# A filler product in front of every transposed score of the 16-dim-head attentions

## The chip, the cores and the metric

The kernel runs on one core of one Trainium2 chip. The metric is the device time of one execution in microseconds (us); several executions are made and their median is compared. The profile is of one further execution.

## The reference, cut to what matters

The program is a decoder of four layers over 4 batches of 512 tokens with 256 features. Each layer has an attention, a cross attention and a feed-forward part, twelve sublayers in all. Three of them (the cross attention of layer 0, the attentions of layers 1 and 3) have 16 heads of 16 dimensions and a softmax over 512 keys; layers 1 and 3 mask the future, layer 0 doesn't. Layer 1 reads:

```python
q, k, v = map(split_heads, (q, k, v))        # 16 heads of 16 dimensions
q = q * dh ** (-0.5)
sim = jnp.einsum('bhid,bhjd->bhij', q, k)
if causal:
    sim = jnp.where(causal_mask, mask_value, sim)
m = jax.lax.stop_gradient(jnp.max(sim, axis=-1, keepdims=True))
e = jnp.exp(sim - m)
num = jnp.einsum('bhij,bhjd->bhid', e, v)
den = jnp.sum(e, axis=-1, keepdims=True) + eps
out = num / den
```

The cross attention of layer 0 divides the scores by 16 and masks nothing; layer 3 rotates q and k first.

## The kernel before, in words

One function, `softmax_heads` (L545), computes these three sublayers. The outer program runs the layers one after the other for a batch in a hardware loop over the four batches, so the trace has twelve calls: the first, third, fifth and seventh without a mask (layer 0), the second, fourth, sixth and eighth causal (layer 1), the last four causal (layer 3, with rotation). Each call is one block in which each engine has a program written out by hand, tied to the others by semaphores.

Heads are taken in eight pairs. A pair lies stacked on the 128 partitions, one head on 64 rows each; q and k are split into a high and a low part, so that a product of 64 rows gives an exact score. For each pair the work has two halves:

- Row scores: `row_scores(p, qt)` (L654) makes, for a tile of 128 queries, the scores against the keys in two products of 64 rows, one for each head, into a ring of three PSUM banks (0 to 2). VectorE takes the row maxima (L785), splits -max in two parts (L795, L797), TensorE transposes them (`put`, L669) and VectorE adds them to q's spare rows (L801).
- Transposed scores: `col_scores(n)` (L682) makes, for a tile of 128 keys, the scores with keys on the partitions and -max already in them, again two products of 64 rows, into banks 3 and 4 or 5 and 6 by turns. ScalarE takes the exp (L880). `weigh(g, kt)` (L701) multiplies by v, four heads side by side in column strips of 32 (p @ v, fp32).

With a mask, products of narrow halves (L659, L687) add the mask's diagonal tile, and the products cover only the columns that count, 128 to 512 of them.

The order on TensorE is that of the loop at L742: for a step i of pair p it issues the row scores of pair p, then the transposed scores of pair p - 2, then p @ v of the step before where that step's pair is an odd one, then, once in a pair, the put. In the first two pairs stacking (L633) and values (L641) take the place of the transposed scores. Behind the last row scores there are eight steps with transposed scores alone, among which the sums (L713), the spreading of 1/sum (L720) and the output projection (L727) are issued.

`col_scores(n)` waits for the exp two steps earlier (`probs_done`, n - 1), which frees the banks that it writes.

A helper, `keep_warm` (L101), issues products whose output nobody reads; it is used in other places of the kernel, among them the tail of each of these calls (L321). Its product is

```python
pe.matmul(self.psum[:, bank, :], self.select[:, 0, :], self.select[:, 0:BANK // P, :], start=True, stop=True)
```

that is 128 rows by 128 columns of weights against 512 columns of a constant, in the type of the stacking products (L633).

Of the kernel before, what the change touches and what calls it, by code (L numbers as in the profile page):

```python
# [544 lines left out]
def softmax_heads(net, W, x, qsrc, ksrc, scale, causal, guard, norm, start, jobs=None, rope=None):  # L545
# [15 lines left out]
    def put_slot(p):  # L561

        return tiles * (p + 1) + p + (PUT_AT if p + 1 < PAIRS else 0)
# [8 lines left out]
    with ExitStack() as ctx:  # L572
# [14 lines left out]
        with net.block() as (block, sem):  # L587
# [34 lines left out]
            def _(pe):  # L622
# [49 lines left out]
                def col_scores(n):  # L672
                    p, kt = divmod(n, steps)
                    if kt == 0:
                        pe.wait_ge(row_read, put_slot(p) + 1)
                    if n >= 2:
                        pe.wait_ge(probs_done, n - 1)
                    else:
                        pe.wait_ge(stacked, outputs)
                    lo = kt * P if causal else 0  # L680
                    for j, half in enumerate(halves):
                        mm = pe.matmul(net.psum[:, 3 + 2 * (n % 2) + j, lo:T], ks[half, p, kt * P:(kt + 1) * P], qs[half, p, lo:T],  # L682
                                       start=True, stop=not causal)
                    if causal:
                        for i in range(2):
                            for j, half in enumerate(halves):
                                mm = pe.matmul(net.psum[:, 3 + 2 * (n % 2) + j, lo:lo + P], net.half_ident[half, i, :],  # L687
                                               net.half_causal_cols[half, i, :], start=False, stop=i == 1)
                    mm.then_inc(colscores_done, 1)
# [52 lines left out]
                for p in range(PAIRS + lag):  # L742
                    for i in range(steps):
                        if p < PAIRS:
                            row_scores(p, i)
                        if p < 2:
                            if i % 2 == 0:
                                stack(2 + 3 * p + i // 2)
                            else:
                                values(2 * p + i // 2)  # L750
                            if i == 3:
                                stack(4 + 3 * p)
                        if p >= lag:
                            n = (p - lag) * steps + i
                            col_scores(n)
                            last_p, last_kt = divmod(n - 1, steps)
                            if n and last_p % 2:
                                weigh(last_p // 2, last_kt)
                        if 1 <= p <= PAIRS and i == (PUT_AT // 2 - 1 if p < PAIRS else 0):
                            put(p - 1)  # L760
                        if p >= PAIRS:
                            at = (p - PAIRS) * steps + i
                            if at in (1, 3, 5):
                                totals(at // 2)
                            if at in (2, 4, 6):
                                spread_inverse(at // 2 - 1)
                            if at in (3, 5, 7):
                                project(at // 2 - 1)
# [1956 lines left out]
```

## Time and profile before

| | |
|---|---|
| median of 3 runs | 4101.51 us (4095.73 to 4104.26) |
| the profiled execution | 4108.26 us |
| its span, first to last instruction | 4106.3 us |
| mean granted TensorE clock | 0.891 |
| TensorE busy | 3326.1 us (81%), 18369 products |
| VectorE busy | 2006.9 us (49%) |
| ScalarE busy | 1238.4 us (30%) |
| GpSimd busy | 427.5 us (10%) |

Busy time of TensorE (PE) counts products from their issue to a modelled end, and neighbouring products overlap, so a high share doesn't say that the array is always streaming. The granted clock is 1.00 at the higher level (2.4 GHz) and 0.50 at the lower; a mean between them says what share of a stretch had which. PEld is the weight load of a product. L numbers are lines of the kernel before. DVE is VectorE, ACT is ScalarE. A timeline line with "x2" merges two products that start within a few ns of each other (one for each head).

### The profile page before, as it was taken

To read this page: it belongs to the slowest core of one execution; us is meant where nothing else is said; L and a number is where in the kernel's file an instruction comes from. 1 tells how busy PE (TensorE), PEld (TensorE's weight loads), DVE (VectorE), ACT (ScalarE), POOL (GpSimd) and SP (SyncE) were. 2 spreads that over 40 slices of the span, in tenths; PEclk is the share of its full clock that TensorE was granted. 3 is DMA by queue.
4 is the path that set the end of the run, shared out by engine and by line. 5 is a ranking of instruction groups with operands and counts; after the bars stand their busy time and mean duration, and the time that the engine had idled before them with its cause. 6 is when DMAs were issued, how large, how long until landed. Compare 5 with 4: busy or idle time off the path is not lost. (4 is left out here: it accounts for less than half of the span.)

```text
span 4106.3 us, 48913 instructions
## 1 busy us (share of the span) xinstructions
PE 3326.1 (81%) x18369; PEld 2148.7 (52%) x18369; DVE 2006.9 (49%) x4645; ACT 1238.4 (30%) x2331; POOL 427.5 (10%) x413
## 2 busy tenths in 40 slices
PE   4878789678869967886996788699496888888888
PEld 2465555436555543655554365555395555454555
DVE  3664446466454646645554564555211535344343
ACT  1413226151322524132252413235131323222132
POOL 1010101111010111001010100101102001010100
PEclk9889899898989988898998889899698999898989
DMA  4000100200010020001002000100585020201101
GB/s 171 6 8 16 76 20 1 90 13 13 22 66 11 1 90 13 13 22 66 11 1 89 13 13 22 66 11 1 206 304 201 1 87 9 87 8 53 43 27 66
DMA packets 53212, 209.29 MB, mean 51 GB/s; under 512 B 4976, under 2 KB 37616, under 8 KB 41328
## 3 DMA queue, kind: packets, MB, share of 16 engines
q1 hardware_dynamic: 48128, 198.85, 13.0%
q0 software_dynamic: 1536, 4.20, 0.3%
q8 instruction: 158, 2.59, 0.3%
q10 hardware_dynamic: 3312, 3.02, 0.2%
q14 instruction: 78, 0.64, 0.1%
HBM read 186.89 MB, written 19.16 MB: 50 GB/s over the span
## 5 line engine op out<-in xcount | busy, mean ns | idle before, releaser
L785 DVE TENSOR_REDUCE nmax<-psum 128x1 f32<-128x512 f32 (+3 forms) x768 | 391.4, 551 | 157.4 <-PE psum L659 124.2
L307 POOL TENSOR_TENSOR rstd<-rstd,consts 128x1 f32<-128x1 f32 x160 | 88.2, 551 | 2204.6 <-DVE rstd L281 2204.6
L880 ACT ACTIVATE probs_odd<-psum 128x1024 f32<-128x1024 f32 x192 | 155.7, 811 | 271.7 <-PE psum L687 189.3
L108 PE MATMUL psum<-select 128*128 128x512 f32 x520 | 192.0, 502 | 49.8 <-PEq L120 49.8
L654 PE MATMUL psum<-ks,qs 64*128 64x512 f32 (+3 forms) x768 | 174.0, 447 | 61.8 <-DVE nmax L785 60.2
L329 ACT ACTIVATE xc<-psum 128x256 f32<-128x256 f32 x144 | 55.4, 385 | 543.6 <-PE psum L314 543.6
L1726 ACT ACTIVATE exps<-exps,nmax 128x512 f32<-128x512 f32 x256 | 183.3, 716 | 71.4 <-DVE nmax L1672 70.9
L1672 DVE CUSTOM_DVE_ANT_0 exps<-psum,mrows 128x512 f32<-128x512 f32 x256 | 166.1, 689 | 67.7 <-PE psum L1619 64.6
L880 ACT ACTIVATE probs_even<-psum 128x1024 f32<-128x1024 f32 x192 | 153.8, 811 | 111.2 <-PE psum L687 74.7
L654 PEld LDWEIGHTS psum<-ks,qs 64*128 64x128 f32 x768 | 75.1, 188 | 201.1 <-DVE nmax L785 120.8
L682 PE MATMUL psum<-qs,ks 64*128 64x512 f32 (+3 forms) x768 | 165.2, 422 | 6.8 <-ACT ks L846 5.9
L701 PE MATMUL psum<-probs_even,v 128*32 128x512 f32 (+3 forms) x768 | 170.2, 523 | 0.0
L701 PE MATMUL psum<-probs_odd,v 128*32 128x512 f32 (+3 forms) x768 | 170.2, 523 | 0.0
L108 PEld LDWEIGHTS psum<-select 128*128 128x128 f32 x520 | 114.7, 239 | 75.8 <-issue 55.6
L314 PE MATMUL psum<-consts,xn 128*128 128x128 f32 x320 | 71.6, 308 | 92.1 <-DVE xn L287 91.9
L1630 PE MATMUL psum<-consts,exps 128*128 128x128 f32 x1024 | 138.9, 279 | 3.9 <-DVE arena L1680 1.5
L1630 PEld LDWEIGHTS psum<-consts,exps 128*128 128x128 f32 x1024 | 109.5, 141 | 56.0 <-ACT exps L1726 39.8
L1641 PE MATMUL psum<-arena,v 128*64 128x512 f32 x512 | 134.8, 608 | 3.6 <-ACT arena L1739 3.2
L727 PE MATMUL psum<-arena,o 128*128 128x256 f32 x384 | 128.9, 494 | 9.3 <-DVE o L828 9.3
L458 PE MATMUL psum<-k,q 128*128 128x512 f32 (+3 forms) x192 | 90.3, 632 | 46.9 <-PEq L120 46.9
L1182 PE MATMUL psum<-qkv_high,xc_parts 128*128 128x512 f32 x384 | 119.2, 390 | 1.3 <-PEq L120 1.3
L2252 PE MATMUL psum<-arena,hidden 128*128 128x256 f32 x512 | 119.6, 379 | 0.0
(395 smaller groups left out, 6987.3 us busy)
## 6 DMA issues: line engine op xcount, KB each, us to landing
arena<-in_w SPq DMA_DIRECT2D x23, 1028.0 KB, 7.7
arena<-in_w SPq DMA_DIRECT2D x23, 1024.0 KB, 7.9
arena<-in_pack_L_ffn SPq DMA_DIRECT2D x4, 5184.5 KB, 15.0
arena<-in_pack_L_xattn SPq DMA_DIRECT2D x4, 4744.0 KB, 14.8
arena<-in_pack_L_ffn SPq DMA_DIRECT2D x4, 4120.0 KB, 12.3
arena<-in_pack_L_attn SPq DMA_DIRECT2D x5, 2432.0 KB, 9.0
arena<-in_pack_L_attn SPq DMA_DIRECT2D x9, 1280.0 KB, 5.7
arena<-ternary SPq DMA_DIRECT2D x4, 2056.0 KB, 7.7
```

What stands on the lines that cost most here:

```text
L108: pe.matmul(self.psum[:, bank, :], self.select[:, 0, :], self.select[:, 0:BANK // P, :], start=True, stop=True)
L654: mm = pe.matmul(net.psum[:, bank_of(s + j), 0:w], qs[half, p, qt * P:(qt + 1) * P], ks[half, p, 0:w], start=True, stop=not causal)
L682: mm = pe.matmul(net.psum[:, 3 + 2 * (n % 2) + j, lo:T], ks[half, p, kt * P:(kt + 1) * P], qs[half, p, lo:T], start=True, stop=not causal)
L701: mm = pe.matmul(net.psum[u * PITCH:(u + 1) * PITCH, 7, lo:T], v[:, kt, 4 * g + u, :], probs((2 * g + u // 2) * steps + kt)[:, u % 2, lo:T ...
L727: mm = pe.matmul(net.psum[:, 1 + t // 2, t % 2 * D:(t % 2 + 1) * D], o[:, g, t * P:(t + 1) * P], W["wo"][:, g * D:(g + 1) * D], start=g == ...
L785: dve.tensor_reduce(nmax[:, p, qt, n % 2:n % 2 + 1], net.psum[:, bank_of(s), 0:w], AX.X, ALU.max, negate=True).then_inc(row_read, 1)
L880: act.activation(probs(n)[:, :, lo:T], net.psum[:, first:first + 2, lo:T], ACT.Exp, scale=scale).then_inc(probs_done, 1)
L1630: mm = pe.transpose(net.psum[:, 4 + j, kt * P:(kt + 1) * P], e[:, m % ring, kt * P:(kt + 1) * P], net.ident)
L1641: mm = pe.matmul(net.psum[half, 6, :], v[:, kt, 2 * p + j, :], turned[p % 2][:, kt, j, :], start=kt == 0, stop=kt == NT - 1, tile_position ...
L1672: dve.tensor_tensor_reduce(e[:, m % ring, :], net.psum[:, 2 * (u % 2) + j, :], mrows[:, u % NT, :], -DK ** -0.5, 1e20, ALU.add, ALU.min, n ...
L1726: act.activation(e[:, m % ring, :], e[:, m % ring, :], ACT.Exp, bias=nmax[:, m % ring:m % ring + 1], scale=-1.0, accum_out=total[:, p % 2, ...
L2252: mm = pe.matmul(output(t), hidden[:, n, t * P:(t + 1) * P], W["up"][:, n * D:(n + 1) * D], start=n == 0 and t % 2 == 0, stop=n == chunks ...
```

## The change

`col_scores` issues one product of `keep_warm` behind its wait and in front of its own products. It is written to the first of the two banks of this step, which the transposed score of the first head overwrites. Nothing else is touched. There are 32 transposed-score steps in a call, so 384 products more in all.

```diff
--- before.py
+++ after.py
@@ -677,6 +677,7 @@
                         pe.wait_ge(probs_done, n - 1)
                     else:
                         pe.wait_ge(stacked, outputs)
+                    net.keep_warm(pe, 1, bank=3 + 2 * (n % 2))
                     lo = kt * P if causal else 0
                     for j, half in enumerate(halves):
                         mm = pe.matmul(net.psum[:, 3 + 2 * (n % 2) + j, lo:T], ks[half, p, kt * P:(kt + 1) * P], qs[half, p, lo:T],
```

## Rows read from the trace of the kernel before

**Rows 1.** Page, part 5: line, engine, operation, tiles, count, busy us, mean ns, idle before

```profile
L682 PE MATMUL psum<-qs,ks 64*128 64x512 f32 (+3 forms) x768 | 165.2, 422 | 6.8 <-ACT ks L846 5.9
```

**Rows 2.** Windows, third call: us, busy us (count) by engine, clock, DMA

```profile
847.10:853.16 6.06, 3.52 (x25) 1.65 (x21) 5.74 (x12) 4.34 (x6) 0.00 (x0) 1.00 0.00 0
853.50:861.00 7.50, 7.50 (x56) 2.24 (x52) 6.29 (x13) 4.10 (x4) 0.00 (x0) 1.00 0.01 2
866.20:869.60 3.40, 3.16 (x14) 0.85 (x14) 2.07 (x4) 1.54 (x2) 0.00 (x0) 0.50 0.00 0
```

**Rows 3.** Timeline, TensorE, third call (not causal): start us, us, line, tiles [idle before]

```profile
847.10 0.50 PE L654 MATMUL psum<-ks,qs 64*128 64x512 f32 x2
...
848.38 0.49 PE L654 MATMUL psum<-ks,qs 64*128 64x512 f32 x2 [0.56 <-DVE nmax L785]
...
849.07 0.63 PE L669 MATMUL psum<-consts,spread 128*128 128x128 f32 x4
850.26 0.49 PE L654 MATMUL psum<-ks,qs 64*128 64x512 f32 x2 [0.56 <-DVE nmax L785]
...
853.16 0.50 PE L654 MATMUL psum<-ks,qs 64*128 64x512 f32 x2 [0.78 <-DVE nmax L785]
853.50 0.40 PE L682 MATMUL psum<-qs,ks 64*128 64x512 f32 x2
853.82 0.62 PE L701 MATMUL psum<-probs_even,v 128*32 128x512 f32 x2
...
854.82 0.50 PE L654 MATMUL psum<-ks,qs 64*128 64x512 f32 x2
```

**Rows 4.** Timeline of TensorE, first call, row scores beside 128-row products

```profile
101.61 0.50 PE L654 MATMUL psum<-ks,qs 64*128 64x512 f32 x2
102.04 0.50 PE L633 MATMUL psum<-xc_parts,select 128*128 128x512 f32 x1
...
102.60 0.39 PE L633 MATMUL psum<-xc_parts,select 128*128 128x512 f32 x1
102.83 0.39 PE L633 MATMUL psum<-low,select 128*128 128x512 f32 x1
103.15 0.50 PE L654 MATMUL psum<-ks,qs 64*128 64x512 f32 x2
```

**Rows 5.** Timeline of VectorE, third call, the step with the put

```profile
850.13 0.68 DVE L801 TENSOR_TENSOR qs<-qs,psum 128x512 fp32r<-128x512 f32 x1
```

**Rows 6.** Groups by line in four waiting steps of the fourth call (causal)

```profile
L654 PE MATMUL psum<-ks,qs 64*128 64x384 f32 (+3 forms) x8 | 1.6, 406 | 1.3 <-DVE nmax L785 1.3
```

**Rows 7.** Timeline of TensorE, third call, a step behind the last row scores

```profile
876.38 1.02 PE L713 MATMUL psum<-consts,o 128*128 128x4 f32 x8 [0.44 <-DVE qs L801]
```

**Rows 8.** Windows, first to twenty-fifth transposed score of each call, and their sum

```profile
833.47:873.42 39.95, 32.31 (x206) 11.73 (x206) 34.99 (x64) 25.00 (x26) 0.00 (x0) 0.96 0.00 1
1042.08:1077.36 35.28, 31.20 (x394) 17.62 (x394) 25.08 (x63) 17.70 (x26) 0.00 (x0) 1.00 0.01 2
1543.44:1586.31 42.87, 35.22 (x207) 12.23 (x208) 35.00 (x64) 25.01 (x26) 0.00 (x0) 0.88 0.00 1
...
sum 453.68, PE 390.91 PEld 191.66 DVE 340.76 ACT 245.37 POOL 0.00; mean PE 32.58 PEld 15.97 DVE 28.40 ACT 20.45 POOL 0.00
```

**Rows 9.** Windows, twenty-fifth to last transposed score of each call, and their sum

```profile
873.42:891.31 17.89, 16.64 (x111) 10.73 (x107) 4.80 (x12) 7.81 (x9) 0.00 (x0) 1.00 0.00 1
1077.36:1099.00 21.64, 20.64 (x138) 14.71 (x134) 5.09 (x13) 5.83 (x8) 0.00 (x0) 0.76 0.00 1
...
1791.85:1812.49 20.64, 19.30 (x138) 13.65 (x135) 5.08 (x13) 5.83 (x8) 0.00 (x0) 0.83 0.00 1
...
sum 244.80, PE 230.90 PEld 160.03 DVE 59.92 ACT 77.46 POOL 0.00; mean PE 19.24 PEld 13.34 DVE 4.99 ACT 6.46 POOL 0.00
```

**Rows 10.** Windows, the 45 us behind the last transposed score of each call

```profile
180.55:225.55 45.00, 27.43 (x113) 19.85 (x113) 22.31 (x71) 12.69 (x17) 15.36 (x9) 0.70 0.08 30
...
1099.00:1144.00 45.00, 37.83 (x146) 23.25 (x146) 16.28 (x40) 7.10 (x16) 4.54 (x5) 0.89 0.13 47
```

## The prediction

> **What bounds the kernel now.** I began with the page's groups to size the edit: the transposed scores are 768 products, two heads to a step, so 384 steps, 32 in each of twelve calls (three attentions, four batches) [rows 1]. The page's shares over the whole span can't say what 384 more products are worth, so I cut the third call, one without a causal mask, into windows. The reader is to see two kinds of step there. In steps without p @ v, VectorE is busy 5.74 us of 6.06 with the row maxima and TensorE 3.52; in steps with p @ v, TensorE is busy 7.50 us of 7.50 [rows 2]. The timeline says the same by waits: before the row scores of the first kind TensorE sat idle 0.56 to 0.78 us until a maximum was taken; in the second kind no row has an idle time [rows 3]. So a longer TensorE step is free in the first kind and lengthens the second by its full amount.
>
> Then the clock. For 3.40 us of this call the grant was 0.50, the lower of its two levels (1.2 GHz) [rows 2]. Over the first 24 steps, a call at 0.96 took 39.95 us and the same call at 0.88 took 42.87 [rows 8]; causal calls mostly hold 1.00 there, at 35.28. In the last eight steps it is the causal calls that fall, to 0.76 and 0.83 [rows 9]. That is what fillers could give back.
>
> **The cost of one filler.** It goes in after the step's existing wait and before its two products, so the same wait now holds the filler's weight load; no wait is added, no DMA, SP or POOL instruction, and the bank is one whose reader that wait covers. ACT's exp and the next p @ v come later by the filler, but exp (one per step) has a whole step before p @ v asks for it.
>
> The price lies in the shape. The filler uses 128 rows; the row scores in front of it and the transposed scores behind it use 64. Same-shape neighbours pack densely: 128-row products stand 0.23 us apart (102.60 to 102.83) [rows 4], and row score to transposed score takes 0.34 (853.16 to 853.50) [rows 3]. Across a change of shape it is 0.43 from the start of a row score to a 128-row product (101.61 to 102.04), and 0.32 from a 128-row product whose load was hidden to the row score behind it (102.83 to 103.15) [rows 4]. The difference, 0.11, is a load that is no longer hidden. With the filler a step reads: row score 0.43, filler 0.32 + 0.11 = 0.43, transposed score 0.32 + 0.11 = 0.43, together 1.29. Now it is 0.66 (853.16 to 853.82) [rows 3]. So **0.63 us** where nothing hides it. The bounds: 0.23, if both loads hide as between equal shapes, and 0.63; I take 0.63, since the rows that put these two shapes side by side all show it. At the lower clock it costs more: the last rival has that.
>
> On this the Trainium skill speaks the other way ("TensorE: Matmul & The Clock Gate", Part 2, Step-by-step): a weight load is pulled ahead of products in flight if it goes to the background buffer. By that alone a filler would cost its 0.23. The trace agrees between equal shapes only; it is the first rival.
>
> **Step by step, full clock.** Of a call's first 24 steps, 11 are followed by p @ v and bound by TensorE: 11 x 0.63 = 6.9 us. The 13 others wait for VectorE. Without a mask, the waits of 0.56 to 0.78 about absorb 0.63, except where -max is put into q: the put starts 0.69 after its row score now (848.38 to 849.07) [rows 3] and at 1.29 after the change, and being 0.63 long would end at 848.38 + 1.29 + 0.63 = 850.30. VectorE's addition, which waits for it, starts at 850.13 now [rows 5]: 0.2 late, once in each of three pairs, 0.6. With the mask, four such steps have only 1.3 us of idle time together [rows 6] against 4 x 0.63 = 2.5: 1.2 at most; starts follow each other closer than the modelled ends that idle time counts from, so I take 0.9, three times: 2.7.
>
> In the last eight steps there are no row scores. The first follows p @ v, whose weights are 32 columns wide: one more shape, 0.43. The other seven follow 128-row products, so only 0.23 is added; three of them stand before a wait like the 0.44 us for VectorE [rows 7] and are free: 4 x 0.23. Together 1.35.
>
> Sum: 6.9 + 0.6 + 1.35 = 8.9 us for each of four calls without a mask, 6.9 + 2.7 + 1.35 = 10.9 for each of eight causal ones: 35.6 + 87.2 = **+123 us**.
>
> **What the clock gives back.** First 24 steps: extrapolating 0.88 and 0.96 to 1.00 gives 42.87 - 12 x 0.365 = 38.5 without a mask; the twelve calls sum to 453.68, less 4 x 38.5 and 8 x 35.28: 17.4 us [rows 8]. Last eight: 17.89 without a mask; causal, 21.64 at 0.76 and 20.64 at 0.83 extrapolate to 18.2; 244.80 - 4 x 17.89 - 8 x 18.2 = 27.6 [rows 9]. So 45 us at most, 0 at least. A filler adds 512 columns to each of the sparse steps. I take all of the 17 (it is mostly the calls without a mask that fall there, those with TensorE busy 3.52 of 6.06 us in the waiting steps [rows 2]) and half of the rest: **-31 us**.
>
> The same page's closing table asks only that TensorE not idle long between bursts if the clock is to hold. By that rule nothing would fall here, where no idle time shown is over 0.78 us, and the gain would be 0. The trace has the falls, and it decides.
>
> Net +92 us. The profiled execution took 4108.26 us (span 4106.3); the median of the runs is 6.75 lower. 4108.3 + 92 = 4200, as a median **4193 us**.
>
> **Rivals.**
> 1. The loads hide after all, and a paid filler costs 0.23. Waiting steps take it free, so 11 + 5 in each call pay: 192 x 0.23 = 44 us; less 31, 4108.3 + 13, as a median 4115 (4101 to 4146 for 45 to 0 recovered). For it: equal shapes do this [rows 4]. Against: the 0.43 beside row scores.
> 2. Faster: the clock. A paid filler at 0.23 breaks even when all 45 us come back (45 / 192 = 0.23), and the gain is decided by whether the clock also holds behind the calls. In the 45 us there it was granted 0.70 to 0.89 [rows 10], so 10 to 27 us at the lower level each, some 220 over twelve. If a quarter of that is spared, that is 55 us at some 0.44 each (2.92 us between 0.88 and 0.96 of 41 us [rows 8], 6.6 us more at the lower level), 24: 44 - 45 - 24 = -25, as a median 4077. Against: the shape price again, and no filler is added behind the calls.
> 3. The filler doesn't do its work: the clock falls as before. Then +123, and the roughly 120 us at the lower level (from the windows' grants) hold some 40 fillers that cost up to twice as much, near +15: +138, as a median 4240. For it: calls whose TensorE is busier than 90% in the last steps still fall [rows 9].
>
> **How the numbers follow.** My forecast (loads exposed, part of the clock back): 0.64, a median of 4165 to 4224. Rival 1: 0.15; rival 2: 0.07; rival 3: 0.14. The range runs from rival 1's middle to rival 3: 4112 to 4240; it leaves out rival 2 and half of rival 1. About 0.2% (8 us) is what a measurement of this kernel can tell from no change. Faster by more: rival 2 and a little of rival 1, 0.08. Within: 0.05, from rival 1. Slower: 0.87.
>
> **What would show it.** 384 more products on line 108. Starts of filler to transposed score 0.43 apart, row score to p @ v 1.29 (0.89 under rival 1). The idle time before row scores in waiting steps nearly gone, that of VectorE in steps with p @ v longer. First 24 steps near 46 us without a mask and near 45 with one, granted clock near 1.00; last eight steps near 19 to 21 us. If row score to p @ v stays near 0.89, the shape price is wrong and with it the sign of the result is open; if the grant in these windows doesn't move, rival 3 holds.

## The result, and the profile after

The changed kernel took 4159.47 us (median; 4150.42 to 4160.94), the kernel before 4099.32 us in the same comparison: a ratio of 1.0141, 95% interval 1.0123 to 1.016. It is slower by 60 us.

From the page of the changed kernel: its span, then groups (line, engine, operation, tiles, count, busy us, mean ns, idle before and what ended it). Behind the edit, lines are one higher.

```profile
span 4158.1 us, 49681 instructions
...
L108 PE MATMUL psum<-select 128*128 128x512 f32 x904 | 383.0, 499 | 54.3 <-PEq L120 48.3
...
L654 PE MATMUL psum<-ks,qs 64*128 64x512 f32 (+3 forms) x768 | 169.3, 436 | 6.5 <-DVE nmax L786 3.9
```

The same groups of the kernel before:

```profile
L108 PE MATMUL psum<-select 128*128 128x512 f32 x520 | 192.0, 502 | 49.8 <-PEq L120 49.8
...
L654 PE MATMUL psum<-ks,qs 64*128 64x512 f32 (+3 forms) x768 | 174.0, 447 | 61.8 <-DVE nmax L785 60.2
```

The products on line 108 went from 520 to 904: the 384 fillers are there. Row scores (L654) had 61.8 us of idle time in front of them and have 6.5. VectorE's idle time before its maxima (L785, now L786) rose from 157.4 to 201.3. What happened to the clock is read from windows of the stage, below.

TensorE in the third call, a call without a mask (start us, duration us, engine, line, operation, tiles, count, idle before):

```profile
852.30 0.50 PE L654 MATMUL psum<-ks,qs 64*128 64x512 f32 x2
852.73 0.50 PE L108 MATMUL psum<-select 128*128 128x512 f32 x1
853.16 0.50 PE L683 MATMUL psum<-qs,ks 64*128 64x512 f32 x2
853.59 0.62 PE L702 MATMUL psum<-probs_even,v 128*32 128x512 f32 x2
...
855.87 0.51 PE L654 MATMUL psum<-ks,qs 64*128 64x512 f32 x2
...
857.16 0.66 PE L669 MATMUL psum<-consts,spread 128*128 128x128 f32 x4
857.76 0.50 PE L654 MATMUL psum<-ks,qs 64*128 64x512 f32 x2
...
859.29 0.51 PE L654 MATMUL psum<-ks,qs 64*128 64x512 f32 x2 [0.17 <-DVE nmax L786]
```

The first four rows are a step followed by p @ v: row score, filler, transposed score and p @ v start 0.43 us apart, 1.29 in all, where [rows 3] had 0.66. The others are steps that used to wait for VectorE: 855.87 to 857.76 goes without a pause, and where a wait is left it is 0.17 (859.29) in place of 0.56 to 0.78 [rows 3].

The weight loads (PEld) of the first of these steps, and below them that of the transposed score in the kernel before:

```profile
852.73 0.19 PEld L108 LDWEIGHTS psum<-select 128*128 128x128 f32 x1 [0.24 <-issue]
853.16 0.19 PEld L683 LDWEIGHTS psum<-qs,ks 64*128 64x128 f32 x2 [0.24 <-issue]
```

```profile
853.26 0.19 PEld L682 LDWEIGHTS psum<-qs,ks 64*128 64x128 f32 x2
```

A load takes 0.19 us. Before, the transposed score's load started 0.24 ahead of its product (853.50 [rows 3]), while the row score was under way. Now the filler's load and the transposed score's start with their products (852.73 and 853.16), 0.24 after the load before them ended: neither is hidden.

The windows answer to [rows 8] and [rows 9] (stretch, its length, busy us and count for PE, PEld, DVE, ACT and POOL, granted clock, DMA). First to twenty-fifth transposed score, then their sum over the twelve calls:

```profile
838.38:884.65 46.27, 45.27 (x231) 17.46 (x230) 35.49 (x65) 25.35 (x26) 0.00 (x0) 1.00 0.00 1
1055.72:1099.11 43.39, 43.07 (x421) 22.54 (x420) 26.21 (x64) 17.85 (x26) 0.00 (x0) 1.00 0.01 1
...
sum 532.17, PE 525.68 PEld 250.04 DVE 351.53 ACT 246.82 POOL 0.00; mean PE 43.81 PEld 20.84 DVE 29.29 ACT 20.57 POOL 0.00
```

Twenty-fifth to last:

```profile
884.65:903.47 18.82, 18.35 (x115) 11.72 (x114) 4.24 (x10) 7.66 (x8) 0.00 (x0) 1.00 0.00 1
1099.11:1117.39 18.28, 17.87 (x143) 12.49 (x143) 4.26 (x11) 5.83 (x8) 0.00 (x0) 1.00 0.00 1
...
sum 221.66, PE 216.41 PEld 146.92 DVE 51.16 ACT 76.91 POOL 0.00; mean PE 18.03 PEld 12.24 DVE 4.26 ACT 6.41 POOL 0.00
```

All twenty-four windows are at a granted clock of 1.00 now (2.4 GHz). The first 24 steps took 532.17 us against 453.68 [rows 8], 78.5 more; the last eight 221.66 against 244.80 [rows 9], 23.1 less. Together +55.4; the span grew by 51.8, so the rest of the program lies within 4 us of what it was. In one and the same change the first part pays and the second part earns. The first stretch ends at the twenty-fifth transposed score, so it also holds the filler in front of that, the first of the last eight steps.

### The profile page after: what moved, and what is told of

Read it like the earlier page. It is cut to its first block and busy times, and to the rows that moved or that the text cites. A ratio compares the mean times of both kernels' runs of the same rounds, so it can differ in the third digit from the quotient of the medians.

```text
span 4158.1 us, 49681 instructions
## 1 busy us (share of the span) xinstructions
PE 3441.8 (83%) x18753; PEld 2190.0 (53%) x18753; DVE 2009.3 (48%) x4645; ACT 1241.1 (30%) x2331; POOL 427.4 (10%) x413
## 5 line engine op out<-in xcount | busy, mean ns | idle before, releaser
L786 DVE TENSOR_REDUCE nmax<-psum 128x1 f32<-128x512 f32 (+3 forms) x768 | 391.3, 551 | 201.3 <-PE psum L659 161.1
L108 PE MATMUL psum<-select 128*128 128x512 f32 x904 | 383.0, 499 | 54.3 <-PEq L120 48.3
L108 PEld LDWEIGHTS psum<-select 128*128 128x128 f32 x904 | 186.0, 217 | 131.6 <-issue 78.6
L329 ACT ACTIVATE xc<-psum 128x256 f32<-128x256 f32 x144 | 55.4, 385 | 540.3 <-PE psum L314 540.3
L654 PE MATMUL psum<-ks,qs 64*128 64x512 f32 (+3 forms) x768 | 169.3, 436 | 6.5 <-DVE nmax L786 3.9
L702 PE MATMUL psum<-probs_odd,v 128*32 128x512 f32 (+3 forms) x768 | 161.1, 498 | 0.0
L702 PE MATMUL psum<-probs_even,v 128*32 128x512 f32 (+3 forms) x768 | 161.1, 498 | 0.0
L654 PEld LDWEIGHTS psum<-ks,qs 64*128 64x128 f32 x768 | 73.4, 185 | 123.5 <-issue 79.0
L728 PE MATMUL psum<-arena,o 128*128 128x256 f32 x384 | 115.6, 453 | 9.4 <-DVE o L829 9.4
L683 PEld LDWEIGHTS psum<-qs,ks 64*128 64x128 f32 x768 | 71.4, 183 | 96.0 <-issue 96.0
```

The costliest lines, as they stand in the source:

```text
L654: mm = pe.matmul(net.psum[:, bank_of(s + j), 0:w], qs[half, p, qt * P:(qt + 1) * P], ks[half, p, 0:w], start=True, stop=not causal)
L702: mm = pe.matmul(net.psum[u * PITCH:(u + 1) * PITCH, 7, lo:T], v[:, kt, 4 * g + u, :], probs((2 * g + u // 2) * steps + kt)[:, u % 2, lo:T ...
L728: mm = pe.matmul(net.psum[:, 1 + t // 2, t % 2 * D:(t % 2 + 1) * D], o[:, g, t * P:(t + 1) * P], W["wo"][:, g * D:(g + 1) * D], start=g == ...
L786: dve.tensor_reduce(nmax[:, p, qt, n % 2:n % 2 + 1], net.psum[:, bank_of(s), 0:w], AX.X, ALU.max, negate=True).then_inc(row_read, 1)
```

## The experiments

All diffs are against the changed kernel. Times are medians, ratios are to the kernel before.

### 64-row fillers in place of 128-row ones

```diff
-                    net.keep_warm(pe, 1, bank=3 + 2 * (n % 2))
+                    for j, half in enumerate(halves):
+                        pe.matmul(net.psum[:, 3 + 2 * (n % 2) + j, :], net.select[half, 0, :], net.select[half, 0:BANK // P, :], start=True, stop=True)
```

> The filler as a pair of 64-row products, one into each of the two banks, so that it has the shape of the row scores before it and of the transposed scores behind it; as many columns stream as before. Theory (most of the price of 0.63 us is the change of shape): row score to p @ v takes 0.34 + 0.23 + 0.32 = 0.89 us in place of 1.29, the first 24 steps take about 41 us without a mask and 38 with one (46.3 and 43.4 with the 128-row filler), the clock stays at 1.00, and the time falls by some 66 us from 4159 to about 4093. Rival (the price is that of a product that writes the bank which the next one overwrites, whatever its shape): step 1.29 or more, 4159 or more. Second rival (64-row pairs don't keep the clock up): step 0.89, but grants near 0.9 again and about 4125.

Measured: 4094.25 us, ratio 0.9994 (0.9985 to 1.0003). TensorE in a step followed by p @ v of the third call (L681 the pair of fillers, L684 the transposed score, L703 p @ v), then the first 24 steps of the third call and of the fourth, a causal one:

```profile
848.62 0.50 PE L654 MATMUL psum<-ks,qs 64*128 64x512 f32 x2
848.96 0.39 PE L681 MATMUL psum<-select 64*128 64x512 f32 x2
849.19 0.40 PE L684 MATMUL psum<-qs,ks 64*128 64x512 f32 x2
849.51 0.62 PE L703 MATMUL psum<-probs_even,v 128*32 128x512 f32 x2
```

```profile
826.27:867.53 41.26, 36.36 (x256) 16.07 (x254) 35.44 (x64) 25.24 (x26) 0.00 (x0) 1.00 0.00 1
1037.29:1075.06 37.77, 36.47 (x444) 20.34 (x442) 25.78 (x62) 17.74 (x26) 0.00 (x0) 1.00 0.01 2
```

Row score to filler 0.34, filler to transposed score 0.23, to p @ v 0.32: 0.89, as the theory gave. The weight load of the transposed score starts ahead of its product again (848.96 to 849.19). The clock is at 1.00 in all calls. The first 24 steps of the twelve calls sum to 467.91 us, 64 less than with the 128-row filler (532.17), for the same streaming in the neighbours' shape: the change of shape was the larger part of the price. A write to the bank that is overwritten next costs nothing that shows: 0.23 is what neighbours of equal shape take in [rows 4].

### One filler of a quarter of the columns, and two fillers

```diff
-                    net.keep_warm(pe, 1, bank=3 + 2 * (n % 2))
+                    pe.matmul(net.psum[:, 3 + 2 * (n % 2), 0:P], net.select[:, 0, :], net.select[:, 0, :], start=True, stop=True)
```

> The 128-row filler with 128 columns in place of 512, in all 32 steps. Theory (0.40 of the 0.63 us is the change of shape, only the streaming shrinks): row score to p @ v about 1.13 us in place of 1.29, so 0.47 for a filler of a quarter of the columns; with the clock at 1.00 some 4128, with the clock falling as before some 4170. Rival (the price goes with the columns): a step of about 0.82 us, 4060 to 4105.

```diff
-                    net.keep_warm(pe, 1, bank=3 + 2 * (n % 2))
+                    net.keep_warm(pe, 2, bank=3 + 2 * (n % 2))
```

> Two 128-row fillers in place of one, in all 32 steps. Theory (the price of the first is mostly the change of shape, a second of the same shape costs its 0.23 us): row score to p @ v 1.52 us in place of 1.29, first 24 steps near 50.5 us without a mask and 48.5 with one, about 4232. Rival (each filler costs 0.63): a step of 1.92 us, over 4330.

Measured, one run each: 4156.17 us with the short filler, 4230.93 us with two. TensorE in a step with p @ v, first with the short filler (L680), then with two (L108, merged into one row):

```profile
853.75 0.50 PE L654 MATMUL psum<-ks,qs 64*128 64x512 f32 x2
854.17 0.33 PE L680 MATMUL psum<-select 128*128 128x128 f32 x1
854.43 0.51 PE L683 MATMUL psum<-qs,ks 64*128 64x512 f32 x2
854.86 0.62 PE L702 MATMUL psum<-probs_even,v 128*32 128x512 f32 x2
```

```profile
865.47 0.49 PE L654 MATMUL psum<-ks,qs 64*128 64x512 f32 x2
865.89 0.73 PE L108 MATMUL psum<-select 128*128 128x512 f32 x2
866.55 0.49 PE L683 MATMUL psum<-qs,ks 64*128 64x512 f32 x2
866.98 0.62 PE L702 MATMUL psum<-probs_even,v 128*32 128x512 f32 x2
```

Row score to p @ v is 1.11 with the short filler and 1.51 with two (865.47 to 866.98), against 1.29 with one and 0.66 with none. So 0.45 for a filler of 128 columns, 0.63 for one of 512, and 0.22 for the second: the price is a fixed part of about 0.40, paid for the change of shape, and the streaming on top. Both rivals, in which the price goes by columns or by fillers, are out.

The short filler's windows hold something else (first 24 steps of the third and fourth call; last eight of the fourth):

```profile
840.51:888.78 48.27, 46.08 (x232) 18.53 (x232) 35.68 (x66) 25.25 (x26) 0.00 (x0) 0.89 0.00 1
1062.20:1102.31 40.11, 39.30 (x420) 22.61 (x419) 25.72 (x62) 17.84 (x26) 0.00 (x0) 1.00 0.01 2
```

```profile
1102.31:1119.92 17.61, 16.67 (x143) 12.50 (x143) 4.47 (x11) 5.83 (x8) 0.00 (x0) 1.00 0.00 1
```

Without a mask the clock still fell: 0.93, 0.89, 0.86 and 0.93 in the four calls, where the kernel before has 0.92, 0.96, 0.88 and 0.88, and the third call took 48.27 us. In the last eight steps it fell in six calls of twelve (nine before). So the step lengthened nearly as the theory said, and less came back: the time was close to the changed kernel's, by another route.

### Fillers in the waiting steps alone

```diff
-                    net.keep_warm(pe, 1, bank=3 + 2 * (n % 2))
+                    if n < 24 and (n == 0 or (n - 1) // steps % 2 == 0):
+                        net.keep_warm(pe, 1, bank=3 + 2 * (n % 2))
```

> The 128-row filler only in the 13 of the first 24 steps that aren't followed by p @ v; none in the other steps and none in the last eight. Theory (there it lies in time in which TensorE waits for VectorE): first 24 steps about 39 us without a mask and 36.5 with one at a clock of 1.00, last eight as in the kernel before (17.9 to 22.2, grants 0.76 to 1.00), together about 4094. Rival (the clock needs the fillers beside p @ v too): without a mask grants of 0.88 to 0.96 as before, about 4110.

Measured: 4135.56 us, ratio 1.0096 (1.0081 to 1.0112). Both numbers for the total were too low. First 24 steps of the third and the fourth call, then the last eight of the third and the sum of the twelve:

```profile
831.98:871.79 39.81, 38.16 (x219) 14.42 (x219) 34.66 (x63) 24.86 (x26) 0.00 (x0) 1.00 0.00 1
1046.33:1084.91 38.58, 36.67 (x408) 19.99 (x407) 25.10 (x62) 17.50 (x26) 0.00 (x0) 1.00 0.01 2
```

```profile
871.79:894.02 22.23, 21.25 (x110) 14.17 (x107) 4.81 (x12) 7.79 (x9) 0.00 (x0) 0.77 0.00 1
...
sum 256.54, PE 242.67 PEld 169.05 DVE 60.02 ACT 77.39 POOL 0.00; mean PE 20.22 PEld 14.09 DVE 5.00 ACT 6.45 POOL 0.00
```

Without a mask it did what was expected: 39.81 us at 1.00, in place of up to 42.87. So the fillers that keep the clock in the first 24 steps are those in the waiting steps; those beside p @ v are not needed for it. With a mask it cost 38.58 against 35.28 [rows 8], 3.3 for three groups of four, 1.1 each, near the upper bound of 1.2. Two stretches of the fourth call show where: four steps with p @ v and the four waiting steps behind them, first in the kernel before, then in this run, with the one wait that this run has there:

```profile
1047.84:1054.56 6.72, 6.62 (x84) 3.33 (x84) 4.44 (x12) 2.85 (x5) 0.00 (x0) 1.00 0.01 2
1054.56:1059.91 5.35, 4.06 (x56) 2.68 (x52) 4.37 (x12) 3.26 (x6) 0.00 (x0) 1.00 0.00 2
```

```profile
1052.72:1059.90 7.18, 6.62 (x90) 3.32 (x88) 4.32 (x12) 2.96 (x5) 0.00 (x0) 1.00 0.01 2
1059.90:1065.89 5.99, 5.89 (x60) 3.51 (x58) 4.51 (x12) 3.03 (x5) 0.00 (x0) 1.00 0.00 1
```

```profile
1054.03 0.62 PE L703 MATMUL psum<-probs_even,v 128*32 128x512 f32 x2 [0.46 <-ACT probs_odd L882]
```

The waiting steps themselves take 0.64 us more (5.99 for 5.35). The other 0.46 stands in front of the first p @ v, which now waits for ScalarE's exp. And in the last eight steps, which have no filler here, the clock fell in all twelve calls, also in those without a mask, where it held in three of four before: 256.54 us in place of 244.80. Why it fell in more of them is not settled.

### Fillers in the last eight steps alone

```diff
-                    net.keep_warm(pe, 1, bank=3 + 2 * (n % 2))
+                    if n >= 24:
+                        net.keep_warm(pe, 1, bank=3 + 2 * (n % 2))
```

> The 128-row filler only in the last eight of the 32 steps of a call. Theory (in these the filler follows 128-row products and costs 0.23 at most, half of it hidden, while the clock there falls in nine calls of twelve): the first 24 steps as in the kernel before (sum 453.7 us over the calls), the last eight 18.8 us without a mask and 18.3 with one at 1.00, sum 222 in place of 244.8: about 23 us less than before, 4076. Rival (the clock in the last eight is decided by what runs before them): grants of 0.76 to 0.83 stay, sum near 255, about 4110.

Measured: 4080.78 us, ratio 0.9965 (0.9952 to 0.9979). First 24 steps of the fourth call, then the sum of the last eight over the twelve calls:

```profile
1036.31:1072.06 35.75, 31.68 (x397) 17.83 (x397) 25.55 (x63) 17.70 (x26) 0.00 (x0) 1.00 0.01 2
```

```profile
sum 221.70, PE 216.46 PEld 146.90 DVE 56.46 ACT 76.91 POOL 0.00; mean PE 18.04 PEld 12.24 DVE 4.71 ACT 6.41 POOL 0.00
```

221.70 us, to within 0.1 of the changed kernel's sum, at 1.00 in all calls. What runs before doesn't decide it; the fillers in these steps do. This part of the change alone is a gain of 0.35%, 15.7 us. The first 24 steps without a mask were granted 0.88 to 0.92 here, 0.88 to 0.96 before. With a mask the fourth call took 35.75 us in them for 35.28 [rows 8], at 1.00 both times: 0.47 is the price of the filler in front of the twenty-fifth transposed score, at which the window ends. Twelve of these are some 5.5 us, so that of the 23.1 us the last eight steps earn about 18.

### Fillers beside p @ v alone

```diff
-                    net.keep_warm(pe, 1, bank=3 + 2 * (n % 2))
+                    if n < 24 and n and (n - 1) // steps % 2:
+                        net.keep_warm(pe, 1, bank=3 + 2 * (n % 2))
```

> The 128-row filler only in the 11 of the first 24 steps that are followed by p @ v. The causal calls hold the clock there with no filler, so they show the price alone. Theory of the prediction (0.63 us in each of these steps, and 0.3 to 1.1 more for four waiting steps, which add up): 35.3 + 6.9 = 42.2 us in the first 24 steps with a mask. Rival (the prices don't add: what the fillers cost in one kind of step is partly time that VectorE uses to get ahead, so it shortens the waiting steps behind it): about 40 us, so that the waiting steps' 3.3 us from the run with fillers there alone and these 4.8 make the 8.1 that the change costs. In total near 4125 to 4145, with grants below 1.00 in the last eight steps.

Measured: 4178.98 us in one run, outside the range that was given. First 24 steps of the third and fourth call:

```profile
847.82:897.74 49.92, 42.29 (x217) 15.10 (x217) 35.75 (x66) 24.98 (x26) 0.00 (x0) 0.90 0.00 1
1069.11:1110.21 41.10, 37.24 (x405) 20.00 (x405) 25.88 (x63) 17.69 (x26) 0.00 (x0) 1.00 0.01 2
```

With a mask 41.10: 5.8 us for eleven fillers, 0.53 each. That lies between the two theories. The two stretches of the fourth call again, in this run, and the second of them in the changed kernel:

```profile
1074.88:1083.66 8.78, 8.78 (x88) 4.17 (x88) 4.64 (x12) 2.83 (x5) 0.00 (x0) 1.00 0.01 2
1083.66:1089.01 5.35, 4.06 (x56) 2.69 (x53) 4.26 (x11) 3.26 (x6) 0.00 (x0) 1.00 0.01 2
```

```profile
1070.90:1076.88 5.98, 5.87 (x60) 3.50 (x58) 4.39 (x11) 3.04 (x5) 0.00 (x0) 1.00 0.00 1
```

Four steps with p @ v take 8.78 us for 6.72, and the waiting steps behind them 5.35, as in the kernel before. So the rival's reason, that VectorE gets ahead and shortens those, is out: 0.63, read from a call without a mask, is about 0.1 too much for a masked step itself. The timeline of these steps shows where. The filler adds 0.50 to 0.58 us between row score and p @ v (0.86 became 1.36 in the first of the four, 0.80 became 1.38 in the third). From the transposed score to p @ v, with the mask's small products between them, it adds 0.03 at most (0.36 before and 0.39 here in the third), where it adds 0.11 without a mask (0.32 and 0.43).

And 5.8 + 3.3 + 0.47 (for the filler in front of the twenty-fifth transposed score) is 9.6, while the changed kernel, which has all of these fillers in the window, pays 8.1. Of the 1.5 between them, 1.4 are the three waits of 0.46 for the exp in the run with fillers in the waiting steps alone. In the changed kernel no p @ v of the twelve calls waits for ScalarE, and four waiting steps cost 0.63 (5.98 for 5.35). Without a mask the clock fell to between 0.81 and 0.90, and the third call took 49.92 us, so these fillers don't hold it.

### Pairs where there is room, and fillers in the last eight

```diff
-                    net.keep_warm(pe, 1, bank=3 + 2 * (n % 2))
+                    if n >= 24:
+                        net.keep_warm(pe, 1, bank=3 + 2 * (n % 2))
+                    elif not causal and (n == 0 or (n - 1) // steps % 2 == 0):
+                        for j, half in enumerate(halves):
+                            pe.matmul(net.psum[:, 3 + 2 * (n % 2) + j, :], net.select[half, 0, :], net.select[half, 0:BANK // P, :], start=True, stop=True)
```

> 64-row pairs only in the 13 waiting steps of the first 24, and only in calls without a mask; the 128-row filler in the last eight steps of all calls. Theory (a pair of equal shape takes 0.23 us out of 0.56 to 0.78 of idle time and so nothing, and the clock holds): without a mask 38.5 to 39 us at 1.00, with one 35.3 to 35.9 as before, last eight 18.8 and 18.3: some 37 us less than before, about 4060. Rival (pairs in the waiting steps alone don't keep the clock up): without a mask grants of 0.88 to 0.96 and 41.5, about 4072.

The other kernel is the same without `not causal and`:

> As the kernel before it in this list, with the pairs in the waiting steps of the causal calls too. Theory: there 0.23 us meets idle times that sum to 1.3 in four steps, so at most 0.3 us for each four, 36 us for the first 24 steps, and no fall of the clock in any call: 4060 to 4066. Rival (the causal steps have no room at all, as the 128-row filler showed with 1.1 us for four): 37.5 us, about 4077.

Measured: 4071.01 us, ratio 0.9931 (0.9918 to 0.9945), and 4073.63 us, ratio 0.9932 (0.9918 to 0.9945). First 24 steps of the third and fourth call with pairs in calls without a mask only:

```profile
826.99:865.78 38.79, 33.90 (x233) 13.92 (x229) 35.09 (x64) 25.23 (x26) 0.00 (x0) 1.00 0.00 1
1035.36:1071.12 35.76, 31.70 (x396) 17.86 (x396) 25.54 (x63) 17.67 (x26) 0.00 (x0) 1.00 0.01 2
```

The fourth call with pairs in all (the third took 38.81 us):

```profile
1034.39:1070.77 36.38, 34.20 (x422) 19.08 (x418) 25.64 (x62) 17.39 (x26) 0.00 (x0) 1.00 0.01 2
```

Without a mask 38.8 us at 1.00: the pairs lie in idle time and cost about nothing against the 38.5 extrapolated for a call at full clock (this window too holds the filler in front of the twenty-fifth transposed score). In the causal calls pairs cost 0.6 us (36.38 for 35.76), and none of the eight fell in the profiled execution, where two fell without them (38.72 at 0.91 in the second call); the two come out the same. Both are faster than the kernel before by 0.7%, a little less than the 37 us expected (29 and 27), and they beat the changed kernel by some 2%. They put the same kind of product only where TensorE waits, or where a change of shape is there anyway.

## Why the prediction was right, and where its terms were off

The prediction was slower, 4193 us in a range of 4112 to 4240; it came to 4159. Sign and range held, but 4159 lies below the band of the main forecast (4165 to 4224). The lower end of that band follows from no term of the sum: with all 45 us of the clock back it gives about 4180.

- **What bounds a step**: right. The fillers lengthen the steps with p @ v, and the waits for VectorE nearly vanish.
- **The price of 0.63 us from the change of shape**: right without a mask, to the hundredth (1.29), and shown by three edits: same shape 0.23, a quarter of the columns 0.45, a second one 0.22. The loads that start with their products, no longer ahead of them, are the mechanism that was named. On rival 1, the Trainium skill's rule ("TensorE: Matmul & The Clock Gate", Part 2, Step-by-step: weight loads are pulled ahead into the background buffer) holds here between equal shapes, at 0.23, and not across shapes, at 0.43.
- **First 24 steps**: 46.3 us measured without a mask (46 forecast), 43.4 with one (45 forecast). Both windows hold the filler in front of the twenty-fifth transposed score, 0.43 in the sum, which the forecast counted with the last eight. So with a mask the fillers cost 8.1 us where the sum has 10.0. That term failed by size in both of its parts: a filler beside p @ v costs 0.53 there and not 0.63, the waiting steps 0.63 for four and not 0.9. The prediction gave the exp a whole step before p @ v asks for it. In the changed kernel that held; with fillers in the waiting steps alone p @ v waited 0.46 for it.
- **Last eight steps**: right. 18.82 without a mask is 0.93 above 17.89 at the same clock, for the seven fillers that this window holds; 1.35 was forecast for all eight, 0.92 of it for these.
- **What the clock gives back**: the term that was off most. I took half of what the last eight steps could return; all of it came, in all twelve calls. And the ceiling was too low: I extrapolated a causal call at full clock to 18.2 us there, while with the short filler it took 17.61 at 1.00, seven fillers included. At full clock the change costs about 4 x (46.27 - 38.5 + 0.93) + 8 x (43.39 - 35.28 + 0.9) = 107 us (0.9 taken over from the calls without a mask), where 123 was forecast; 107 - 55 = 52 us came back, where 31 was forecast. The two errors don't cancel: both make the forecast loss too large, by 37 together; the span grew by 51.8, and the forecast was 92.
- **Rival 3**, that the clock falls as before, is out: 1.00 in all twenty-four windows. **Rival 2** had the clock's part in these windows nearly right (45 us) and the price wrong. The 24 us that it saw behind the calls didn't come: all that lies outside the windows changed by 3.6 us.
- The rule in the closing table of the same page of the Trainium skill (TensorE must not idle long between bursts) would have left the gain at nothing. The falls with idle times under 0.8 us, and their end where fillers stand in the waiting steps, speak against it as a sufficient rule.

## What to carry to other kernels

A filler isn't priced by its columns alone: look at the shape of the products on both sides of it, because a change of shape exposes a weight load on each side (0.43 us from product to product in place of 0.23). Put fillers where the engine waits anyway, in the neighbours' shape, and leave them out of steps that the engine bounds. When the clock is at stake, split the stage and read length and grant of each part: here one part of the edit earned some 18 us and the other paid some 73, and the total showed neither.

## What the runs showed that I had not expected

Fillers beside p @ v alone left the clock worse than no fillers. In the one execution profiled, the four calls without a mask were granted 0.81, 0.90, 0.90 and 0.87 (0.92, 0.96, 0.88 and 0.88 before), and the third took 49.92 us for a stretch that takes 38.8 at full clock with pairs in it. By lengths and grants, some 54 us of these four stretches were at the lower level, where it had been 30. With the short filler in every step it was 38, too near to 30 to tell from one execution of each. Yet full-size fillers in the waiting steps alone held 1.00 in every call. Where the clock falls also moved between stretches: in the run with fillers in the waiting steps alone, the last eight steps fell in all calls. What decides which stretch falls is open; it was not tried apart.
